# Causal attention: the next unit's transposes go ahead of the output projection on TensorE

## The chip, the cores and the metric

One NeuronCore of a Trainium2 chip runs the whole program. TensorE (PE) multiplies and transposes into PSUM, VectorE (DVE), ScalarE (ACT) and GpSimd (POOL) do the element-wise work, SyncE (SP) issues most DMAs. The engines run their own instruction streams in order and meet at semaphores. The metric is the device time in microseconds of one execution, the median of the runs.

## The reference, cut to what matters

A decoder of two layers with layer norms behind each sublayer, on x of 32 sequences x 128 rows x 256 features. Only the causal attention of the second layer is touched:

```
q = einsum('btm,mhd->bhtd', x, wq); k = ... wk; v = ... wv      # 2 heads of 128
q = frac_rope(q) * 128 ** -0.5;  k = frac_rope(k) * 128 ** -0.5
s = einsum('bhid,bhjd->bhij', q, k), masked above the diagonal
o = einsum('bhij,bhjd->bhid', softmax(s), v)
x = layernorm(x + einsum('bhid,hdm->bim', o, wo))
```

Before it stands x = layernorm(x + experts(x)): two gathered expert rows for each row, weighted and added, then the norm. This is done in the same stage.

## The kernel before

The program is a sequence of stages; each engine has one function per stage. The stage in question has `c_sync`, `c_gpsimd`, `c_tensor`, `c_scalar` and `c_vector`. The work is cut into 16 units (UNITS) of two sequences, 256 rows each. `pipelined` calls `step(t)` for t = 0 to 20 on every engine (lag 5; the steps 8 to 15 are two rounds of a loop with four steps in its body, the others are written out). In a step an engine works on several units at once: `t.at(k, UNITS)` is unit t - k, or nothing where there is none. The order of an engine's work is the order of the `if` blocks in its `step`, written out by hand; there is no planner.

Unit n goes through the stage like this. Step n: x2 is loaded (L1368) and POOL issues four gathers of expert rows (L1414). Step n+1: VectorE mixes them (L1599) into C["r"] and takes the moments; POOL takes the root (L1394, L1396); ScalarE writes the normalised rows C["x3"] (L1403, called in the u0 block; the u4 block uses the same line for the stage's result x4). Step n+2: TensorE turns x3 into bank 0 (`to_feature`, four transposes, L490), ScalarE copies them to C["x3F"] (L1532), TensorE projects queries (bank 1), keys (bank 2, both L1454) and values (bank 3, L1509); VectorE and POOL do the rope (L1592 to L1594, L1410), ScalarE copies the values (L1577). Step n+3: mask and scores (L1480, L1486), maximum (L1632), exponential (L1557), reciprocal of the sum (L1644), weights normalised (L1571). Step n+4: TensorE turns the weights (L1468), ScalarE copies them (L1536), weights times values (L1501, bank 6), ScalarE's copy C["oF"] (L1551), output projection (L1517, bank 7). Step n+5: VectorE adds the residual (L1609) and takes the moments, then root and ScalarE's normalised result, which SP stores.

So TensorE's order in a step is: turn of x3, turn of weights, queries, scores, keys, weights times values, values, output projection. ScalarE's is: copy of turned x3, copy of turned weights, x4, upper half of the queries (L1543), x3, oF, exponential, upper half of the keys (L1566), normalised weights, values. VectorE's is: residual and moments of the unit five back, mix and moments of the newest, rope of the queries, maximum, rope of the keys, reciprocal.

`done(eng, sem, u)` waits until unit u has passed the semaphore; the turn of x3 waits for `c_x3` (the rows) and for `c_x3F` of the unit before (bank 0 emptied), the copy L1532 for `c_x3T` (the turn) and for `c_v` of the unit before (x3F read).

Of the kernel before, what the change touches and what calls it, by code (L numbers as in the profile page):

```python
# [23 lines left out]
ACT = mybir.ActivationFunctionType  # L24
# [7 lines left out]
UNITS = B // UB  # L32
# [134 lines left out]
def pipelined(eng, count, lag, step, unroll=2, peel=0, first=0, tail=None):  # L167


    head = lag + 2  # L170
    head += (count - head) % unroll
    for t in range(first, head):
        step(Unit(0, t, unroll))
    with eng.Fori(0, (count - head - peel) // unroll) as i:
        for j in range(unroll):
            step(Unit(i, head + j, unroll))
    for t in range(count - peel, count + (lag if tail is None else tail)):
        step(Unit(0, t, unroll))


def done(eng, sem, u, per=1):

    if u.fixed and u.n < 0:
        return
    eng.wait_ge(sem, (u.n + 1) * per)
# [16 lines left out]
def decoder(nc, a, where, out):  # L202
    ctx = ExitStack()
    with ctx:
# [5 lines left out]
        def sem(name):  # L210
            in_use.append(nc.alloc_semaphore(name))
            return in_use[-1]
# [6 lines left out]
        def bank(k):  # L219
            return psum[:, k, :]  # L220
# [265 lines left out]
        def to_feature(dst, src):  # L486

            for c in range(NC_):
                for b in range(UB):
                    ins = nc.tensor.transpose(dst[:, c * T + b * S:c * T + (b + 1) * S],  # L490
                                              src[:, b, c * P:(c + 1) * P], ident)
            return ins
# [17 lines left out]
        def chunks(ap):  # L510
            return ap.rearrange("p (c t) -> p c t", c=NC_)
# [7 lines left out]
        def seqs(ap):  # L519
            return ap.rearrange("p (b d) -> p b d", b=UB)  # L520
# [775 lines left out]
        C = {}  # L1296
        for n in ("x2", "v", "x4"):
# [20 lines left out]
        c_idx, c_mix, c_x3T, c_q, c_k, c_v, c_S, c_pT, c_o, c_wo = (  # L1318
            sem("c_" + n) for n in ("idx", "mix", "x3T", "q", "k", "v", "S", "pT", "o", "wo"))
        c_x3F, c_q2, c_k2, c_vs, c_ex, c_pTs, c_os = (  # L1320
            sem("c_" + n) for n in ("x3F", "q2", "k2", "vs", "ex", "pTs", "os"))
# [4 lines left out]
        c_x3, c_x4 = ln3[3], ln4[3]  # L1326
# [15 lines left out]
        def kv_rest_tensor(pe):  # L1342
            for k in range(KV_REST):
                pe.wait_ge(kr_in[k], 16)
                done(pe, kr_s, Unit(0, k - 2), 2)
                project_features(bank(4 + 2 * (k % 2)), "L1_xattn_Wk", KV["cF_rest"][:, k])
                project_rows(bank(5 + 2 * (k % 2)), "L1_xattn_Wv", KV["cF_rest"][:, k]).then_inc(kr_p, 1)
            pe.wait_ge(kr_s, 2 * KV_REST)
# [97 lines left out]
        def c_tensor(pe):  # L1446
            kv_rest_tensor(pe)

            def project(u, k, name, s_out, read):
                for r in read:  # L1450
                    done(pe, r, u.back(1))
                for h in range(H1):
                    for c in range(NC_):
                        ins = nc.tensor.matmul(bank(k)[:, h * T:(h + 1) * T], w[name][:, c, h * P:(h + 1) * P],  # L1454
                                               C["x3F"][:, c, :], start=(c == 0), stop=(c == NC_ - 1))
                ins.then_inc(s_out, 1)

            def step(t):
                u1, u2, u3 = (t.at(k, UNITS) for k in (2, 3, 4))
                if u1:  # L1460
                    done(pe, c_x3, u1)
                    done(pe, c_x3F, u1.back(1))
                    to_feature(bank(0), C["x3"][:, u1.c % 4]).then_inc(c_x3T, 1)
                if u3:
                    done(pe, c_p, u3)
                    done(pe, c_pTs, u3.back(1))
                    for n in range(UB * H1):
                        ins = nc.tensor.transpose(bank(5)[:, n * S:(n + 1) * S], C["e"][:, u3.p, n, :], ident)  # L1468
                    ins.then_inc(c_pT, 1)
                if u1:  # L1470
                    done(pe, c_x3F, u1)
                    project(u1, 1, "L1_attn_wq", c_q, (c_qt, c_q2))
                if u2:
                    done(pe, c_qr, u2)
                    done(pe, c_kr, u2)
                    done(pe, c_q2, u2)
                    done(pe, c_k2, u2)
                    done(pe, c_ex, u2.back(1))

                    nc.tensor.matmul(bank(4), ident_bf[:, :],  # L1480
                                     causal_bf[:, None, :].broadcast_to([P, UB * H1, S]), start=True, stop=False,
                                     skip_group_check=True)
                    for b in range(UB):
                        for h in range(H1):
                            n = b * H1 + h
                            ins = nc.tensor.matmul(bank(4)[:, n * S:(n + 1) * S],  # L1486
                                                   C["q"][:, u2.p, h, b * S:(b + 1) * S],
                                                   C["k"][:, h, b * S:(b + 1) * S], start=False,
                                                   stop=(n == UB * H1 - 1), skip_group_check=True)
                    ins.then_inc(c_S, 1)  # L1490
                if t.fixed and t.n == UNITS + 2:
                    e_turn(pe, Unit(0, 0, 4), 0)
                if u1:
                    project(u1, 2, "L1_attn_wk", c_k, (c_kt, c_k2))
                if u3:
                    done(pe, c_pTs, u3)
                    done(pe, c_vs, u3)
                    done(pe, c_os, u3.back(1))
                    for b in range(UB):
                        for h in range(H1):  # L1500
                            ins = nc.tensor.matmul(bank(6)[:, h * T + b * S:h * T + (b + 1) * S],  # L1501
                                                   C["v"][:, u3.p, b, h * P:(h + 1) * P],
                                                   C["pT"][:, b * H1 + h, :], start=True, stop=True)
                    ins.then_inc(c_o, 1)
                if u1:
                    done(pe, c_vs, u1.back(1))
                    for b in range(UB):
                        for c in range(NC_):
                            ins = nc.tensor.matmul(bank(3)[:, b * D:(b + 1) * D], C["x3F"][:, c, b * S:(b + 1) * S],  # L1509
                                                   w["L1_attn_wv"][:, c, :], start=(c == 0), stop=(c == NC_ - 1))  # L1510
                    ins.then_inc(c_v, 1)
                if u3:
                    done(pe, c_r4, u3.back(1))
                    done(pe, c_os, u3)
                    for b in range(UB):
                        for h in range(H1):
                            ins = nc.tensor.matmul(bank(7)[:, b * D:(b + 1) * D], C["oF"][:, h, b * S:(b + 1) * S],  # L1517
                                                   w["L1_attn_wo"][:, h, :], start=(h == 0), stop=(h == H1 - 1))
                    ins.then_inc(c_wo, 1)
                if t.fixed and t.n == UNITS + 2:  # L1520
                    e_query(pe, Unit(0, 0, 4), 1)
            pipelined(pe, UNITS, C_LAG, step, unroll=4)

        def c_scalar(act):
            kv_rest_scalar(act)

            def step(t):
                u0, u1, u2, u3, u4 = (t.at(k, UNITS) for k in (1, 2, 3, 4, 5))
                if u1:
                    done(act, c_x3T, u1)  # L1530
                    done(act, c_v, u1.back(1))
                    nc.scalar.activation(C["x3F"], chunks(bank(0)), ACT.Copy).then_inc(c_x3F, 1)  # L1532
                if u3:
                    done(act, c_pT, u3)
                    done(act, c_o, u3.back(1))
# [38 lines left out]
                if u1:  # L1574
                    done(act, c_v, u1)
                    done(act, c_o, u1.back(2))
                    nc.scalar.activation(C["v"][:, u1.p], seqs(bank(3)), ACT.Copy).then_inc(c_vs, 1)  # L1577
                if t.fixed and t.n == UNITS + 2:
                    e_take_query(act, Unit(0, 0, 4), 1)
                if t.fixed and t.n == UNITS + 3:  # L1580
# [199 lines left out]
        def e_turn(pe, u, k):  # L1780
            landed(pe, x_in, u, 2)
            to_feature(bank(k), X["x4"][:, u.p]).then_inc(x_xT, 1)

        def e_query(pe, u, k):
            done(pe, x_xF, u)
            project_features(bank(k), "L1_xattn_Wq", X["x4F"]).then_inc(x_q, 1)
# [737 lines left out]
```

## Time and profile before

| | us |
|---|---|
| median of 3 runs (lowest to highest) | 1630.32 (1626.74 to 1630.99) |
| the profiled execution: time | 1628.0 |
| the profiled execution: span, first to last instruction | 1626.0 |

| engine | busy us in the span | share |
|---|---|---|
| PE (matmuls) | 1494.3 | 92% |
| DVE | 1123.7 | 69% |
| ACT | 823.3 | 51% |
| POOL | 603.2 | 37% |

The busy times cover six stages with different limits. The stage of the change fills roughly the stretch from 728 us (first turn of x3) to 924 us (last residual add), about an eighth of the span. Within it the idle time just before an instruction and what ended it (the groups, the timeline) say who waits for whom, and the chain of waits, followed back from the last instruction, says which of these waits are passed on to the end.

### The profile page before, as it was taken

Reading aid. Unit: us, or ns where it says so; the run is one execution under the profiler, and the core shown is the slowest. Engines: PE = TensorE matmul, PEld = TensorE weight load, DVE = VectorE, ACT = ScalarE, POOL = GpSimd, SP = SyncE. Lnnn points to the kernel's source line nnn. Section 1 sums busy time; section 2 is a strip of 40 time slices with the busy share of each in tenths; the row PEclk is TensorE's granted clock in tenths of the full one; section 3 lists DMA queues with packets and bytes.
Section 4 is the critical chain, followed back from the end, with each engine's and each line's share of the span. In section 5 each row is a group of like instructions: output and inputs, shape, how many; then the busy total and the mean of one; then the engine's idle time right before and its main releaser. Section 6 shows DMA issues by size and latency. Waiting matters only on the chain.

```text
span 1626.0 us, 34497 instructions
## 1 busy us (share of the span) xinstructions
PE 1494.3 (92%) x12742; PEld 1341.2 (82%) x12742; DVE 1123.7 (69%) x2334; ACT 823.3 (51%) x1559; POOL 603.2 (37%) x700
## 2 busy tenths in 40 slices
PE   4888889899999999978999789999979999989997
PEld 2777777799999999957778568888869999979997
DVE  3899987756555556317889448888766676757684
ACT  5777742245444544425777546656524444434442
POOL 3666651222012111027887213313114444434443
PEclk9999999899999999988999879999989999989999
DMA  6222253203233331062333132222136445363533
GB/s 192 66 79 77 71 189 109 97 27 101 95 104 103 97 97 40 14 210 79 94 91 115 58 133 80 70 68 77 35 75 126 99 102 125 84 126 68 118 76 73
DMA packets 118159, 152.11 MB, mean 94 GB/s; under 512 B 10090, under 2 KB 102852, under 8 KB 117508
## 3 DMA queue, kind: packets, MB, share of 16 engines
q1 hardware_dynamic: 110068, 127.48, 28.5%
q0 software_dynamic: 6560, 19.02, 4.1%
q10 hardware_dynamic: 1392, 3.70, 0.6%
q8 instruction: 94, 1.54, 0.4%
q14 instruction: 45, 0.37, 0.1%
HBM read 111.37 MB, written 38.80 MB: 92 GB/s over the span
## 4 chain that ended last, share of the span: by engine, by line
PE 36%; issue 7%; DVE 6%; DMA 3%; ACT 2%; POOL 2%; SPq 1%; DVEq 0%; POOLq 0%; ACTq 0%
PE psum L531 14%; PE psum L1880 4%; PE psum L506 3%; PE psum L498 3%; PE psum L1857 2%; PE psum L1454 2%; PE psum L1848 2%; DMA arena_x<-wT_d 1%; POOL d_g_parts L2236 1%; PE psum L1517 1%; PE psum L1835 1%; PE psum L1842 1%; PE psum L490 1%; PE psum L1509 1%; DVE psum L2465 1%
## 5 line engine op out<-in xcount | busy, mean ns | idle before, releaser
L2236 POOL TENSOR_TENSOR d_g_parts<-arena_w,d_g_parts 128x512 fp32r<-128x512 f32 x128 | 166.2, 1299 | 247.0 <-ACT d_g_parts L2368 246.8
L531 PE MATMUL psum<-d_v_high,d_g_parts 128*128 128x256 f32 x1024 | 205.5, 284 | 4.7 <-DVE arena_x L2006 3.2
L531 PE MATMUL psum<-d_x_parts,d_v_high 128*128 128x256 f32 x1024 | 194.4, 287 | 8.5 <-issue 7.1
L531 PE MATMUL psum<-m_w_high,m_h_parts 128*128 128x256 f32 x1024 | 188.0, 284 | 0.0
L1213 ACT ACTIVATE arena_x<-psum,b_e 128x512 f32<-128x512 f32 x128 | 88.3, 690 | 189.3 <-PE psum L531 88.8
L1141 POOL DMA_INDIRECT arena_x<-x_d,slot_row x64 | 67.1, 1049 | 293.0 <-PE psum L1187 228.5
L531 PEld LDWEIGHTS psum<-d_v_high,d_g_parts 128*128 128x128 f32 x1024 | 168.7, 192 | 5.5 <-issue 4.7
L531 PEld LDWEIGHTS psum<-d_x_parts,d_v_high 128*128 128x128 f32 x1024 | 160.0, 192 | 15.5 <-issue 9.7
L531 PE MATMUL psum<-m_xF_parts,m_w_high 128*128 128x512 f32 x512 | 159.5, 393 | 2.1 <-DVE m_xF_parts L526 2.1
L531 PEld LDWEIGHTS psum<-m_w_high,m_h_parts 128*128 128x128 f32 x1024 | 160.7, 192 | 0.0
L2376 ACT ACTIVATE arena_y<-psum 128x512 f32<-128x512 f32 x128 | 76.2, 596 | 152.7 <-PE psum L531 152.4
L2465 DVE SCALAR_TENSOR_TENSOR psum<-arena_y,psum 128x512 f32<-128x512 f32 x128 | 88.4, 691 | 87.3 <-ACT arena_y L2376 87.0
L531 PE MATMUL psum<-d_x_parts,d_vd_low 128*128 128x256 f32 x512 | 145.3, 284 | 0.0
L531 PE MATMUL psum<-d_vu_low,d_g_parts 128*128 128x256 f32 x512 | 145.3, 284 | 0.0
L531 PE MATMUL psum<-m_w_low,m_h_parts 128*128 128x256 f32 x512 | 144.8, 283 | 0.0
L2368 ACT ACTIVATE d_g_parts<-arena_w 128x512 fp32r<-128x512 f32 x128 | 80.4, 628 | 71.0 <-DVE arena_w L2471 71.0
L526 DVE TENSOR_TENSOR m_h_parts<-arena_x,m_h_parts 128x512 fp32r<-128x512 f32 x128 | 84.6, 686 | 43.8 <-ACT m_h_parts L1217 43.8
L531 PEld LDWEIGHTS psum<-m_xF_parts,m_w_high 128*128 128x128 f32 x512 | 96.0, 190 | 21.8 <-issue 2.5
L2471 DVE TENSOR_TENSOR arena_w<-psum,arena_x 128x512 f32<-128x512 f32 x128 | 88.4, 691 | 27.5 <-DMA arena_x<-wT_d 22.8
L1948 ACT ACTIVATE arena_x<-psum,arena_x 128x1024 f32<-128x1024 f32 x64 | 71.2, 1113 | 57.8 <-PE psum L1857 55.6
L531 PE MATMUL psum<-m_xF_parts,m_w_low 128*128 128x512 f32 x256 | 100.4, 392 | 0.0
L2031 DVE TENSOR_REDUCE arena_x<-psum 128x8 f32<-128x1024 f32 x64 | 78.0, 1220 | 29.9 <-PE psum L1848 29.8
(281 smaller groups left out, 3768.4 us busy)
## 6 DMA issues: line engine op xcount, KB each, us to landing
arena_x<-wT_d SPq DMA_DIRECT2D x128, 256.0 KB, 5.7
arena_y<-in_L_ffn_w SPq DMA_DIRECT2D x16, 1024.0 KB, 7.9
x_d<-arena_x SPq DMA_DIRECT2D x32, 256.0 KB, 2.2
y_d<-arena_x SPq DMA_DIRECT2D x16, 512.0 KB, 9.1
arena_x<-kv_d SPq DMA_DIRECT2D x16, 512.0 KB, 3.6
kv_d<-arena_x SPq DMA_DIRECT2D x9, 512.0 KB, 3.0
arena_x<-in_x SPq DMA_DIRECT2D x16, 256.0 KB, 2.9
arena_x<-in_ctx SPq DMA_DIRECT2D x16, 256.0 KB, 3.0
```

Of the source, the lines that this page charges most:

```text
L526: return nc.vector.tensor_tensor(dst, src, high.bitcast(F32), ALU.subtract)
L531: ins = nc.tensor.matmul(dst, left[a_], right[b_], start=start and k == 0, stop=stop and k == 2, skip_group_check=True)
L1141: nc.gpsimd.indirect_dma_start(out=M["x"][:, u.p, q, :], out_offset=None, in_=x2_d.rearrange("b s d -> (b s) d"), in_offset=bass.IndirectO ...
L1213: nc.scalar.activation(M["hr"][:, m % 4, :], bank(2 + m % 4), ACT.Relu, bias=b1_e[:, (u.c // 2) % 2, m:m + 1]).then_inc(m_hs, 1)
L1880: ins = nc.tensor.matmul(bank(7)[32 * quad:32 * quad + 32, (kind * NC_ + c) * S:(kind * NC_ + c + 1) * S], left, X["eT"][:, b, at:at + S], ...
L1948: nc.scalar.activation(X["eT"][:, b, half * 1024:(half + 1) * 1024].rearrange("p (q n) -> p q n", q=2), psum[:, 4:6, :], ACT.Exp, scale=HD ...
L2031: nc.vector.tensor_reduce(X["mx"][:, b, :].rearrange("p (q j) -> p q j", q=4)[:, quads_, 0:4], psum[:, quads_, :].rearrange("p q (k s) -> ...
L2236: nc.gpsimd.tensor_tensor(K["gP"][:, s % 4, 1], K["g"][:, s % 2], K["gP"][:, s % 4, 0].bitcast(F32), ALU.subtract).then_inc(d_gl, 1)
L2368: nc.scalar.activation(K["gP"][:, s % 4, 0], K["g"][:, s % 2], ACT.Copy).then_inc(d_gh, 1)
L2376: nc.scalar.activation(K["th"][:, s % 2], bank(2 + s % 4).rearrange("p (k t) -> p k t", k=2), ACT.Tanh, scale=0.5).then_inc(d_th, 1)
L2465: nc.vector.scalar_tensor_tensor(z, K["th"][:, s % 2].rearrange("p k t -> p (k t)"), 1.0, z, ALU.add, ALU.mult).then_inc(d_t, 1)
L2471: nc.vector.tensor_tensor(K["g"][:, s % 2], z, K["w"][:, s // 4, 2 * (s % 4):2 * (s % 4) + 2, :] .rearrange("p k t -> p (k t)"), ALU.mult) ...
```

## The change

On TensorE the block that turns x3 leaves the head of the step, where it served unit t - 2, and stands now behind the value projection and ahead of the output projection, where it serves unit t - 1. On ScalarE the block that copies the turned rows leaves the head of the step and stands behind the value copy, for unit t - 1. Each unit is thus turned and copied in step n+1 and not in step n+2. The waits are the same, of the same units. Buffers, banks, the other engines and all DMAs are as before.

```
@@ c_tensor, step(t)
-                u1, u2, u3 = (t.at(k, UNITS) for k in (2, 3, 4))
-                if u1:
-                    done(pe, c_x3, u1)
-                    done(pe, c_x3F, u1.back(1))
-                    to_feature(bank(0), C["x3"][:, u1.c % 4]).then_inc(c_x3T, 1)
+                u0, u1, u2, u3 = (t.at(k, UNITS) for k in (1, 2, 3, 4))
                 if u3:
                     done(pe, c_p, u3)
@@ behind the value projection
                     ins.then_inc(c_v, 1)
+                if u0:
+                    done(pe, c_x3, u0)
+                    done(pe, c_x3F, u0.back(1))
+                    to_feature(bank(0), C["x3"][:, u0.c % 4]).then_inc(c_x3T, 1)
                 if u3:
                     done(pe, c_r4, u3.back(1))
                     done(pe, c_os, u3)
@@ c_scalar, step(t)
-                if u1:
-                    done(act, c_x3T, u1)
-                    done(act, c_v, u1.back(1))
-                    nc.scalar.activation(C["x3F"], chunks(bank(0)), ACT.Copy).then_inc(c_x3F, 1)
@@ behind the value copy
                     nc.scalar.activation(C["v"][:, u1.p], seqs(bank(3)), ACT.Copy).then_inc(c_vs, 1)
+                if u0:
+                    done(act, c_x3T, u0)
+                    done(act, c_v, u0.back(1))
+                    nc.scalar.activation(C["x3F"], chunks(bank(0)), ACT.Copy).then_inc(c_x3F, 1)
```

## Rows read from the trace of the kernel before

**Rows 1.** Busy time of each engine, 740 to 895 us, TensorE's granted clock, DMA share, GB/s.

```profile
740.00:895.00 155.00, 141.69 (x772) 120.97 (x770) 134.81 (x375) 111.44 (x300) 122.52 (x169) 0.98 0.33 96
```

**Rows 2.** Groups, 740 to 895 us: busy us, mean ns | idle before us <-releasers.

```profile
L1454 PE MATMUL psum<-arena_y,arena_w 128*128 128x256 f32 x218 | 54.8, 395 | 5.3 <-ACT arena_y L1532 5.3
...
L1609 DVE TENSOR_TENSOR arena_y<-psum,arena_y 128x512 f32<-128x512 f32 x13 | 9.0, 691 | 8.4 <-PE psum L1517 8.4
L1468 PE MATMUL psum<-arena_w,arena_y 128*128 128x128 f32 x52 | 9.0, 298 | 8.0 <-ACT arena_y L1571 7.9
...
L1532 ACT ACTIVATE arena_y<-psum 128x512 f32<-128x512 f32 x13 | 7.7, 591 | 0.0
```

**Rows 3.** Chain of waits, 800 to 850 us: start us, us, what.

```profile
807.52 1.99 PE psum L1454 x8
...
809.73 0.89 PE psum L1486 x8
810.62 1.73 PE psum L1454 x8
812.35 0.89 PE psum L1501 x8
813.24 1.73 PE psum L1509 x8
814.97 1.74 PE psum L1517 x8
...
816.74 0.70 DVE arena_y L1609
...
826.95 0.19 DVE arena_y L1644
...
829.06 0.50 ACT arena_y L1532
...
829.60 1.99 PE psum L1454 x8
```

**Rows 4.** Chain of waits: three more starts of the query projection.

```profile
762.97 1.99 PE psum L1454 x8
...
852.02 1.99 PE psum L1454 x8
...
896.40 1.99 PE psum L1454 x8
```

**Rows 5.** Timeline, 811 to 820 us: start us, us, engine line [idle before <-releaser].

```profile
812.12 1.09 ACT L1403 ACTIVATE arena_y<-arena_y,C_st 128x256 f32<-128x256 f32 x2 [1.98 <-POOL C_st L1396]
...
813.28 0.60 ACT L1551 ACTIVATE arena_y<-psum 128x512 f32<-128x512 f32 x1
...
814.81 1.89 PE L1517 MATMUL psum<-arena_w,arena_y 128*128 128x256 f32 x8
...
816.54 0.60 PE L490 MATMUL psum<-arena_w,arena_y 128*128 128x128 f32 x4
...
817.49 0.66 PE L1468 MATMUL psum<-arena_w,arena_y 128*128 128x128 f32 x4 [0.35 <-ACT arena_y L1571]
817.96 0.59 ACT L1532 ACTIVATE arena_y<-psum 128x512 f32<-128x512 f32 x1
```

**Rows 6.** Timeline, 904 to 910 us: the four transposes between other matmuls.

```profile
907.72 0.60 PE L490 MATMUL psum<-arena_w,arena_x 128*128 128x128 f32 x4
...
908.16 1.06 PE L1501 MATMUL psum<-arena_y 128*128 128x128 f32 x8
```

**Rows 7.** Chain of waits, 878 to 965 us: the stage's end and the next stage's start.

```profile
903.85 1.74 PE psum L1517 x8
...
937.95 7.86 DMA arena_x<-kv_d
```

**Rows 8.** VectorE's mix L1599, 750 to 890 us: its idle time before, us, times, until.

```profile
L1599 DVE SCALAR_TENSOR_TENSOR arena_y<-arena_y,gates x51: 471/479/493, 749.6 to 886.6; 128x256 f32<-128x256 f32 x51
...
  issue: 1.1, 4
```

## Prediction

> **What bounds the kernel now.** The change touches one stage of six, the causal attention of the second layer, so I read that stage and not the shares of the whole span. Between 740 and 895 us TensorE is busy for 141.69 of 155 us at a mean granted clock of 0.98, VectorE for 134.81, POOL for 122.52, ScalarE for 111.44 [rows 1]. No engine is full, so the order decides, and the next view is the list of idle times. There the reader is to see four entries. VectorE waits 13 times, 8.4 us in all, for the last output projection matmul (L1517) before it can add the residual (L1609). TensorE waits 5.3 us for ScalarE's copy of the turned rows (L1532) before it projects the queries (L1454), and 7.9 us for the weights' normalisation (L1571) before it turns the weights (L1468). The copy L1532 itself waits for nothing: 0.0 us in 13 instances [rows 2]. So the thing that this change brings forward, the turn that feeds L1532, is not late in any of these steps.
>
> The chain of waits says how the waits join. It runs: query projection at 807.52, then scores, keys, P times V, values and output projection, each starting where the one before it ends, to 816.71 (814.97 + 1.74), VectorE's residual add at 816.74, then VectorE's queue in order (moments, mix of the gathered rows, rope products) to the reciprocal at 826.95, ScalarE's normalisation and value copy, its copy of the turned rows at 829.06, and query projection again at 829.60 [rows 3]. That is one round, 22.08 us, and it spans two steps: the projection of step t releases the queries of step t+2. Two such rounds are interleaved, one for even and one for odd steps. Other starts of the same line give the mean: from 762.97 to 896.40 there are 12 steps, 11.12 us each, so 22.24 us a round; 852.02 less 829.60 is 22.42 [rows 3, 4].
>
> **The change, part by part.** *TensorE.* The four transposes of a unit (L490) now stand behind the step's output projection; they go ahead of it. They were the first thing of step t+1 and become the last but one of step t, so on TensorE they move past exactly one thing, the eight matmuls L1517. Nothing is added or taken away, and no DMA or queue of SP or POOL is moved.
>
> What the turn costs where it stands: nothing. In the timeline the projection's eight matmuls begin at 814.81, the turn at 816.54, and after it TensorE idles 0.35 us until ScalarE's normalisation ends and L1468 can start at 817.49 [rows 5]. Taking the turn away from there gives nothing, since this wait is ended by ScalarE, not by TensorE's queue. The query projection behind it does not come sooner either: its copy L1532 starts at 817.96, right behind the value copy, whatever TensorE did [rows 5].
>
> What it costs in its new place: TensorE is gapless from the query projection to the end of the output projection [rows 3], so the projection ends later by the turn's length. Price of a turn between other matmuls: another turn of the same form, which stands between the scores and the value product, starts at 907.72 and the next matmul at 908.16, so 0.44 us for four [rows 6]. Bounds: four times 0.11 as just read, which I take, and 0.60, the turn's own busy time with its pipeline's end in it [rows 5]. The Trainium skill, "TensorE: Matmul & The Clock Gate", Part 4, puts a PE-mode transpose at about 275 ns in a kernel's context; that would be an estimated 1.1 us for a turn and 6.6 us in the sum below, and 1636.9 us in place of my time. This trace has a mean of about 0.27 us for the duration of one, but the next instruction starts 0.11 us later, and the sum goes by starts.
>
> *The turn's waits.* It waits for the next unit's normalised rows (L1403). In the step of rows 5 these two instructions start at 812.12 and take 1.09 us, so they end at 813.21, while the value projection hands over to the output projection at 814.97 [rows 3, 5]: 1.7 us of slack. Queued behind this wait is now the output projection, but that needs ScalarE's copy L1551 (813.28, 0.60 us), which stands behind L1403 in ScalarE's own order [rows 5]. So whatever holds the turn would hold the projection anyway; the wait adds nothing. The turn's other wait, that bank 0 has been emptied, is for a copy at the start of the same step.
>
> *ScalarE.* The copy goes from the head of step t+1 to the tail of step t. Between the value copy and the next copy (L1536) nothing else stands, so the order of its instructions over the stage is unaltered: value copy, turned rows, turned weights. It already starts without waiting [rows 2]. Gain and loss: 0. Only the place of the loop's back edge changes, between two instructions that follow each other without a gap.
>
> *The sum.* Steps with both a turn and a projection: the first output projection is in the fifth step (t = 4), the last turn in step t = 16, so 13 of the 16 turns are moved ahead of a projection. But a delay enters a round only once in two steps. The odd round passes the projections of t = 5, 7, 9, 11, 13, 15 and arrives at the last query projection (896.40) [rows 4]: 6 x 0.44 = 2.6 us. The even round passes seven, 3.1 us, and ends in a step where VectorE idles for the projection of the odd one. From there on no turn stands ahead of a projection and the 2.6 us are carried: projection at 903.85, then after the stage's last results the next stage's key and value loads at 937.95 [rows 7], both on the chain. Later stages are the same code.
>
> What can take a part of it off: VectorE's mix of the gathered rows starts late by 1.1 us in four instances between 750 and 890, by waits that the profile puts down to issue [rows 8]; where that is a gather still in flight, a round stretched elsewhere hides it. Shared by two rounds this is 0.5 to 1.1 us at most. I leave it out of the sum and keep it for the lower bound, 1.5 us.
>
> Profiled execution: span 1626.0 us, time 1628.0; with the change 1628.6 and 1630.6. The median of the three runs is 2.3 us above that profiled time, so the forecast is 1630.3 + 2.6 = 1632.9 us, 0.16% slower, which a measurement of this kernel cannot tell from no change (it tells about 0.3%, 4.9 us).
>
> **Rivals.**
> (a) *One-step round.* If VectorE's own sequence, or the turn of the weights, hands the delay on in each step and not in each second one, all 13 turns count: 13 x 0.44 = 5.7 us, 1636.0 us, slower. It decides from 0.38 us a step on (4.9 / 13). For it: VectorE is busy 134.81 of 155 us [rows 1], so few pauses are left in which its queue could catch up. Against it: it does pause, 8.4 / 13 = 0.65 us in every step right before the residual add [rows 2], and TensorE pauses before L1468 and L1454.
> (b) *Nothing moves.* The gathers, not the projection, set the pace: each gather waits for POOL, the mix waits for the gather, POOL waits for the mix, and this loop goes round in one step. If this loop sets the 11.12 us a step now and the two-step round has 0.22 us a step to spare, the delay vanishes in it: 1630.3 us. For it: the 1.1 us [rows 8]. Against: only four pauses in more than twelve steps, and the chain goes past them.
> (c) *The queries come sooner.* If the copy were released earlier by the turn, TensorE's 5.3 us before L1454 [rows 2] would go, all of it more than paying for the turn: 1630.3 - 5.3 = 1625.0 us, if the delay does not count as well. Against: L1532 has no idle time before it.
> (d) The turn costs more than 0.44 us between two long runs of 256-column matmuls: at 0.60 the sum is 3.6 us, 1633.9, at 1.1 us (four durations of a transpose) 6.6 us, 1636.9.
>
> **How the numbers follow.** Forecast, with (d) up to 0.6 us a turn: 0.60. (b): 0.14. (a), with the dearer (d) and a granted clock that falls in some other place: 0.19. (c): 0.07. Within 0.3% lie the forecast, (b) and the near ends of the others: 0.72. Slower by more: 0.20. Faster by more: 0.08. The range: below, (b) and the scatter of the three runs, which reach 3.6 us below their median, 1627.5; above, (a) and (d), 1637.0. What is left out are (c) and the tails.
>
> **What the profile will show.** If the steps are right: L490's four stand between L1509 and L1517; VectorE's idle time before L1609 grows; TensorE's before L1468 grows by less than 0.44 us a step; L1532 still idles 0.0; L1454's starts are about 11.34 us apart instead of 11.12; the stage's last query projection is 2.6 us later. The prediction is wrong if L1454's starts stay at 11.1 (b), go to 11.5 and more (a), or if L1454 no longer waits for L1532 (c).

## The result, and the profile after

The change makes the kernel a little slower: 1631.86 us (median of 20 runs, 1628.42 to 1643.15) against 1628.71 us (20 runs, 1623.52 to 1634.23); ratio 1.0028, 95% interval 1.0014 to 1.0041. The difference of the medians is 3.2 us, the ratio says 4.6 us; both are slower, and small. The forecast was 2.6 us slower (1632.9 us). The profiled execution has a span of 1630.9 us, 4.9 us above that of before.

In the tables of the changed kernel the value projection is L1505, the turn of the weights L1464, ScalarE's copy of the turned rows L1577, its value copy L1573, its normalisation L1567, its exponential L1553; the turn of the rows (L490) and the output projection (L1517) kept their numbers. First the chain of waits between 815 and 835 us, which answers to [rows 3] (start us, us, what):

```profile
817.44 0.97 ACT arena_y L1567 x3
...
818.43 0.60 ACT arena_y L1573
819.03 0.50 ACT arena_y L1577
...
819.57 1.99 PE psum L1454 x8
...
825.29 1.73 PE psum L1505 x8
827.02 0.44 PE psum L490 x4
827.46 1.74 PE psum L1517 x8
829.20 0.02 issue
829.23 0.70 DVE arena_y L1609
```

The reader is to see one new line, L490 x4 with 0.44 us, between the value projection and the output projection, on the chain. From the query projection's start to the projection's end it is 9.63 us (827.46 + 1.74 - 819.57) where it was 9.19 [rows 3]. What ScalarE does ahead of the query projection (normalisation, value copy, copy of the turned rows) is the same, in the same order. The groups between 740 and 900 us (busy, mean ns | idle before <-releaser) answer to [rows 2]:

```profile
L1454 PE MATMUL psum<-arena_y,arena_w 128*128 128x256 f32 x216 | 55.5, 402 | 5.6 <-ACT arena_y L1577 5.6
...
L1464 PE MATMUL psum<-arena_w,arena_y 128*128 128x128 f32 x56 | 9.6, 297 | 10.8 <-ACT arena_y L1567 10.4
L1609 DVE TENSOR_TENSOR arena_y<-psum,arena_y 128x512 f32<-128x512 f32 x13 | 9.0, 691 | 12.2 <-PE psum L1517 12.2
...
L1577 ACT ACTIVATE arena_y<-psum 128x512 f32<-128x512 f32 x14 | 8.3, 592 | 0.0
```

VectorE's wait for the output projection rose from 8.4 to 12.2 us (13 adds in both: 0.65 to 0.94 us each). TensorE's for the normalised weights rose from 7.9 us in 13 steps to 10.4 us in 14, 0.61 to 0.74 us each. The query projection still waits for the copy (5.6 us), and the copy, whose turn now comes early, still waits 0.0 us: it had nothing to gain.

One thing was not forecast. TensorE's part of the timeline between 838 and 848 us:

```profile
838.17 1.89 PE L1517 MATMUL psum<-arena_w,arena_y 128*128 128x256 f32 x8
841.22 0.65 PE L1464 MATMUL psum<-arena_w,arena_y 128*128 128x128 f32 x4 [1.16 <-ACT arena_y L1567]
842.43 3.31 PE L1454 MATMUL psum<-arena_y,arena_w 128*128 128x256 f32 x8 [0.56 <-ACT arena_y L1577]
845.54 0.63 PE L1476 MATMUL psum<-causal_bf,ident_bf 128*128 128x512 bf16 x1
```

The query projection of step 12 (unit 10) takes 3.31 us instead of 1.99. In the windows (stretch, its length, busy us of PE, PEld, DVE, ACT, POOL, granted clock, DMA share, GB/s) the clock of that stretch is 0.92:

```profile
740.00:762.00 22.00, 18.65 (x90) 15.35 (x89) 15.84 (x39) 12.90 (x38) 15.43 (x19) 0.84 0.25 73
828.00:850.00 22.00, 19.68 (x102) 16.25 (x101) 18.76 (x54) 14.11 (x35) 17.85 (x26) 0.92 0.32 91
```

In the kernel before the same stretch is granted 1.00:

```profile
828.00:850.00 22.00, 20.30 (x114) 17.39 (x113) 19.64 (x56) 16.23 (x44) 18.30 (x27) 1.00 0.34 96
```

I split each profiled execution at instructions whose first and last start a line's own view gives. "Steps 5 to 17" is the time from ScalarE's copy of the turned rows that the query projection of step 5 needs to the copy that step 17's needs, twelve periods; "stage" is from its first such copy to VectorE's last residual add (L1609); "next" from there to the first L2465 of the last stage; "last" from the first to the last L2465. All in us:

| kernel | steps 5 to 17 | one step | stage | next | last | span |
|---|---|---|---|---|---|---|
| before | 133.42 | 11.12 | 194.2 | 275.3 | 412.4 | 1626.0 |
| the change | 137.92 | 11.49 | 197.6 | 275.3 | 414.2 | 1630.9 |

Of the 4.9 us the stage has 3.4: 4.5 in the twelve steps, and 1.0 back behind the last of them, from 27.8 to 26.8 us. That 1.0 us is one instruction group, the stage's last output projection, which runs at half clock for its whole length before (granted clock 0.50 between 919.77 and 923.50 us) and for a part of it after the change (0.68 between 923.81 and 926.60 us; first line before, second line the change):

```profile
919.77 3.75 PE L1517 MATMUL psum<-arena_w,arena_y 128*128 128x256 f32 x8 [2.91 <-ACT arena_y L1551]
923.81 2.79 PE L1517 MATMUL psum<-arena_w,arena_y 128*128 128x256 f32 x8 [2.91 <-ACT arena_y L1547]
```

The stage of the change also begins 0.4 us sooner in its profiled execution. Another 1.8 us are in the last stage, which the change does not touch and which differs from one profiled kernel to the next (below).

### The profile page after: what moved, and what is told of

It is laid out like the page before. It is cut to its first block, busy times and chain, and to the rows that moved or that the text cites. A ratio compares the mean times of both kernels' runs of the same rounds, so it can differ in the third digit from the quotient of the medians.

```text
span 1630.9 us, 34503 instructions
## 1 busy us (share of the span) xinstructions
PE 1494.4 (92%) x12742; PEld 1339.6 (82%) x12742; DVE 1125.1 (69%) x2334; ACT 822.1 (50%) x1559; POOL 602.4 (37%) x700
## 4 chain that ended last, share of the span: by engine, by line
PE 36%; DVE 7%; issue 5%; DMA 4%; ACT 2%; POOL 2%; SPq 1%; DVEq 0%; ACTq 0%; POOLq 0%
PE psum L531 14%; PE psum L1880 4%; PE psum L506 3%; PE psum L498 3%; DMA arena_x<-wT_d 2%; PE psum L1857 2%; PE psum L1454 2%; PE psum L1848 2%; DVE psum L2465 1%; PE psum L490 1%; PE psum L1835 1%; PE psum L1842 1%; PE psum L1517 1%; DMA wT_d<-arena_w 1%; PE psum L1505 1%
## 5 line engine op out<-in xcount | busy, mean ns | idle before, releaser
L531 PEld LDWEIGHTS psum<-d_x_parts,d_v_high 128*128 128x128 f32 x1024 | 160.2, 193 | 16.2 <-issue 10.4
L2465 DVE SCALAR_TENSOR_TENSOR psum<-arena_y,psum 128x512 f32<-128x512 f32 x128 | 88.4, 690 | 87.2 <-ACT arena_y L2376 87.0
```

What stands on the lines that cost most here:

```text
L531: ins = nc.tensor.matmul(dst, left[a_], right[b_], start=start and k == 0, stop=stop and k == 2, skip_group_check=True)
L2465: nc.vector.scalar_tensor_tensor(z, K["th"][:, s % 2].rearrange("p k t -> p (k t)"), 1.0, z, ALU.add, ALU.mult).then_inc(d_t, 1)
```

## The experiments

All ratios are against runs of the kernel before on the same chip, with their 95% intervals. In the kernels called filled, TensorE does transposes that nobody uses, in every step or (early) in the first steps alone; they are explained below, under the granted clock.

| kernel | time, ratio (interval) | steps 5 to 17 | one step | stage | next | last |
|---|---|---|---|---|---|---|
| TensorE's part alone | 1.0022 (1.0004 to 1.0040) | 137.96 | 11.50 | 197.7 | 275.3 | 413.4 |
| ScalarE's part alone | 1.0001 (0.9985 to 1.0016) | 133.44 | 11.12 | 194.1 | 275.4 | 417.6 |
| the turn three times | 1.0023 (1.0005 to 1.0042) | 141.69 | 11.81 | 198.9 | 276.7 | 407.8 |
| projection ahead of values | 1.0010 (0.9993 to 1.0028) | 136.45 | 11.37 | 197.3 | 275.4 | 410.7 |
| copy ahead of values | 0.9980 (0.9966 to 0.9994) | 133.77 | 11.15 | 191.4 | 272.6 | 413.2 |
| queries first | 0.9946 (0.9932 to 0.9959) | 130.94 | 10.91 | 188.1 | 272.3 | 411.7 |
| change, filled | 1.0040 (1.0025 to 1.0054) | 136.27 | 11.36 | 194.6 | 276.9 | 414.7 |
| before, filled | 0.9944 (0.9927 to 0.9961) | 133.43 | 11.12 | 191.7 | 272.3 | 407.7 |
| before, filled early | 0.9912 (0.9890 to 0.9933) | 133.45 | 11.12 | 191.8 | 272.2 | 408.0 |
| change, filled early | 0.9972 (0.9956 to 0.9988) | 136.27 | 11.36 | 194.6 | 272.6 | 408.6 |
| queries first, filled early | 0.9910 (0.9893 to 0.9928) | 130.17 | 10.85 | 186.0 | 278.1 | 406.2 |

### The two halves of the change

TensorE's block moved, ScalarE's left, and the other way round.

> Only TensorE's part of the change: the turn for unit t-1 ahead of the output projection, ScalarE's copy at the head of its step as before. Theory (the turn lengthens a round that spans two steps): same as the whole change, 2.6 to 3.1 us above before, query projections 11.36 us apart where the granted clock stays full, first query projection with an output projection in the step before it to the last one 3.0 us longer than before's 133.4 us. Rival (ScalarE's copy at its new place costs something): 0 to 1 us above before.

> Only ScalarE's part: the copy of the turned rows stands behind the value copy of the step before, TensorE as before. Theory: ScalarE's instructions follow each other in the same order, so 0 us, within 0.5 us of before, query projections 11.12 us apart. Rival (the place of the copy counts): it carries a good part of the 3 us.

The first gives 137.96 us for the twelve steps, the change 137.92; the second 133.44, before 133.42. The cost is TensorE's alone and ScalarE's move is worth nothing. The first shows the slow step 12 as well, with the granted clock at 0.92 between 828 and 850 us, so this is no accident of one execution. The times agree with it: ratio 1.0022 for TensorE's half, 1.0001 for ScalarE's.

### A larger dose: the turn three times

```
                 if u0:
                     done(pe, c_x3F, u0.back(1))
+                    to_feature(bank(0), C["x3"][:, u0.c % 4])
+                    to_feature(bank(0), C["x3"][:, u0.c % 4])
                     to_feature(bank(0), C["x3"][:, u0.c % 4]).then_inc(c_x3T, 1)
```

> The whole change, with the four transposes done three times over in the same place (eight transposes more in each step, the result is the same). Each step's output projection ends another 0.88 us later. Theory (two-step round): 6 x 0.88 = 5.3 us above the change, 8 to 9 us above before, query projections 11.36 + 0.44 = 11.8 us apart. Rival (a), every step passes the delay on: 13 x 0.88 = 11.4 us above the change, 12.2 us apart. Rival (b), the gathers set the pace: under 2 us above the change. If TensorE's own work becomes the limit (about 9.6 + 0.9 us and its two waits) the time lies between theory and rival (a).

TensorE's timeline (here L1519 is the output projection), one step, and the window around the first steps:

```profile
815.14 1.89 PE L1505 MATMUL psum<-arena_w,arena_y 128*128 128x256 f32 x8
816.87 1.47 PE L490 MATMUL psum<-arena_w,arena_y 128*128 128x128 f32 x12
818.18 1.89 PE L1519 MATMUL psum<-arena_w,arena_y 128*128 128x256 f32 x8
```

```profile
740.00:762.00 22.00, 19.08 (x113) 16.77 (x114) 16.79 (x41) 13.08 (x39) 17.27 (x23) 1.00 0.25 73
```

Twelve transposes take 1.31 us between starts, 0.11 each. A step takes 11.81 us, what the two-step round says (11.80), and not 12.2: rival (a) falls, and so does (b), since the gathers do not hide the growth. (11.80 is 11.36, a step of the change at full clock, and half of 0.88.) Yet the whole is hardly slower than the change, where 5.3 us more were expected. With the added transposes the granted clock is also higher in the first steps, 1.00 instead of 0.84, so the period of step 4 to 5 is 10.84 us and not 13.18, that of step 2 to 3 is 7.44 and not 8.31, and step 12 is not slow. The dose's cost, 5.4 us, stands in the steps, and a gain of another kind, 2.3 + 0.9 + 1.65 us, stands against it; with 0.8 us more behind the last step, the stage is 1.3 us longer than the change's. The last stage of this execution is 6.4 us shorter than the change's, in code that is the same. Judged by the time alone this run would have spoken for rival (b).

### The output projection ahead of the values

Kernel before, the two blocks exchanged on TensorE.

> The kernel before, with the output projection ahead of the value projection: the 1.73 us of the value projection leave the round, but the projection then waits for ScalarE's copy, which ends 0.6 us behind the product that it copies. Theory: the projection ends about 1.0 us sooner, 6 rounds, 5 to 6 us faster than before, unless the value projection, now last, holds ScalarE's value copy up (its slack is about 0, so 3 to 4 us are the lower estimate). Rival (a): 13 x 1.0 = 13 us faster at most. Rival (b): no change.

```profile
826.54 0.60 ACT L1551 ACTIVATE arena_y<-psum 128x512 f32<-128x512 f32 x1 [0.88 <-PE psum L1501]
827.28 1.97 PE L1510 MATMUL psum<-arena_w,arena_y 128*128 128x256 f32 x8 [0.78 <-ACT arena_y L1551]
829.08 1.89 PE L1517 MATMUL psum<-arena_w,arena_y 128*128 128x256 f32 x8
831.01 0.60 ACT L1577 ACTIVATE arena_y<-psum 128x512 f32<-128x512 f32 x1 [0.55 <-PE psum L1517]
```

Here L1510 is the output projection and L1517 the value projection. My lower estimate, 3 to 4 us gained, was wrong: steps take 11.37 us, regular, and the time is the same within its interval. The projection now waits 0.78 us for ScalarE's copy, and ScalarE's value copy 0.55 us for TensorE, which it never did before. That closes a round of one step: value projection, value copy, copy of the turned rows, query projection, and TensorE's queue through ScalarE's copy L1551 and the output projection back to the value projection. It takes 11.37 us, longer than half of the old two-step round (11.12). The slack that I had called about 0 was what decided.

### What the earlier turn makes possible

ScalarE copies the turned rows ahead of the values (first kernel), and ahead of the normalised weights, with TensorE's query projection ahead of its turn of the weights (second kernel):

```
 c_scalar, first kernel               c_scalar, second kernel
   normalised weights (u2)            + copy of turned rows (u0)
 + copy of turned rows (u0)             normalised weights (u2)
   value copy (u1)                      value copy (u1)
 - copy of turned rows (u0)           - copy of turned rows (u0)
 c_tensor, second kernel
 + queries (u1)
   turn of weights (u3)
 - queries (u1)
```

> The whole change, and ScalarE copies the turned rows ahead of the values (the turn is now ready by then). Theory (two-step round, ScalarE's value copy lies in it): 0.5 us less for a round, so the query projections are 11.36 - 0.25 = 11.1 us apart where the clock is full, 3.0 us less than the change, about the time of before, 0 to 1.5 us above it. Rival (the query projection is held by something else, the turn of the weights on TensorE): as the change.

> The whole change, and ScalarE copies the turned rows ahead of the normalised weights, and TensorE projects the queries ahead of the turn of the weights, so that the query projection hangs on the turn of the rows and no longer on the softmax. Theory: the query projection leaves the round (about 2 us less of 22.7), until another bound shows: VectorE's own step of 10.5 us or TensorE's own 10.1 us. Query projections 10.6 to 10.8 us apart, the stage 5 to 8 us shorter than before, 1622 to 1625 us. Rival (a one-step round through ScalarE shows up, as in the kernel with the output projection ahead of the values): 11.1 to 11.4 us apart, no gain.

The first: 11.15 us a step, 0.21 less than the change at full clock (11.36), 0.25 expected. The time was expected 0 to 1.5 us above the kernel before and came out 3.2 us below it, ratio 0.9980. The steps 5 to 17 do not give that (133.77 us against 133.42). In the profiled execution 2.3 us come in the steps before them, 0.9 us behind them and 2.7 us in the unchanged next stage. The period of step 4 to 5 is 11.46 us where the change has 13.18, and the query projection of step 4 takes 2.82 us where it takes 3.78 in the kernel before and in the change, with the granted clock at 0.92 and not 0.84 between 740 and 762 us, though nothing was filled in:

```profile
751.42 2.82 PE L1454 MATMUL psum<-arena_y,arena_w 128*128 128x256 f32 x8
```

The second, between 762 and 890 us and in its timeline (L1567 is the copy of the turned rows, L1467 the turn of the weights, L1571 the normalisation):

```profile
L1454 PE MATMUL psum<-arena_y,arena_w 128*128 128x256 f32 x188 | 45.7, 386 | 7.9 <-ACT arena_y L1567 7.9
...
L1532 ACT ACTIVATE arena_y<-psum 128x512 f32<-128x512 f32 x11 | 6.6, 597 | 10.1 <-PE psum L1467 10.1
```

```profile
823.20 0.60 ACT L1567 ACTIVATE arena_y<-psum 128x512 f32<-128x512 f32 x1
...
823.69 1.27 ACT L1571 ACTIVATE arena_y<-arena_y 128x128 f32<-128x128 f32 x4
823.85 1.99 PE L1454 MATMUL psum<-arena_y,arena_w 128*128 128x256 f32 x8 [0.54 <-ACT arena_y L1567]
...
825.68 0.60 PE L1467 MATMUL psum<-arena_w,arena_y 128*128 128x128 f32 x4
```

The query projection starts beside the normalisation, not behind it, and the turn of the weights finds them ready. 10.91 us a step (10.6 to 10.8 expected) and 1618.9 us (1622 to 1625 expected), ratio 0.9946: faster than both kernels. The stage is 6.1 us shorter than before's; 2.5 of that are in the twelve steps, the rest in the first steps, where the clock is better too (0.92), and 3.0 us more are in the unchanged next stage. The move that cost 2.8 us by itself stands here in a kernel whose steps are shorter than before's, once what stands behind the turn is moved up with it. Whether that gain needs the turn's new place was not tested: no run moves the copy and the query projection and leaves the turn where it was. What now remains is again a wait for the copy, 7.9 us over the window, and ScalarE's pause of 10.1 us for the turned weights.

### The granted clock

Unused turns into bank 5 behind the place of the output projection. Filled: one in each step that has a turn and three in the steps below 4; filled early: three in the steps below 4 alone. In the kernel before the condition is u1, so its first filled step is step 2, in the change (u0) it is step 1; the doses of the first steps differ by that.

```
                     ins.then_inc(c_wo, 1)
+                if u0:                       # filled early: and t.fixed and t.n < 4
+                    for _ in range(3 if t.fixed and t.n < 4 else 1):
+                        to_feature(bank(5), C["x3"][:, u0.c % 4])
```

> The whole change, with one more turn (four transposes, not used) behind the output projection in each step, three in the first steps, where TensorE waits anyway. Theory (of the change's 4.4 us in the stage 3.0 are the turn ahead of the projection and 1.4 a stretch at half the granted clock in step 12): the clock is 1.00 from 762 us on, the stretch goes, the query projections stay 11.36 us apart, and the half clock near 750 us goes too, as in the kernel with three turns: stage 3 to 5 us shorter than the change's, time near or below before's. Rival (the clock has nothing to do with it): no gain against the change, or a loss of up to 0.4 us a step.

> The kernel before with the same filling behind its output projection, for the turn alone at equal clock. Theory: 11.12 us apart as before, half clock near 750 us gone, stage 2 to 3 us shorter than before's, and shorter than the filled change by the turn's 2.6 to 3.0 us. Rival: filling costs TensorE 0.44 us a step and the pauses don't cover it, 0 to 3 us slower than before.

> The kernel before with three unused turns behind the place of the output projection in the first steps (t < 4) alone, where TensorE stands and the granted clock falls. Theory: step 4's queries at full clock, query projections then 11.12 us apart; attention stage 191.7 us against 194.2. If the whole time falls by far more than these 2.5 us, as it did with filling in every step (9.9 us), the rest lies in the stages behind, and the trace says in which; rival: the rest was the filling of the later steps, and this kernel gains 2.5 us only.

> The whole change with the same filling in the first steps alone. Theory (the stretch at half clock in step 12 belongs to the change's longer pauses in the later steps): it stays, query projections 11.49 us apart on average, stage 195.5 to 196.5 us, 4 to 4.5 us longer than with the filled kernel before. Rival (that stretch depends on what happened near 750 us): it goes or moves, 11.36 us apart, stage 194.6 us.

> The kernel with the queries ahead of the turn of the weights, and the filling in the first steps. Theory: its steps are 10.85 us apart at full clock already, so only the first steps gain: 0.5 to 2 us in the stage, 186 to 187.5 us; whole time 1617 to 1619 us, the fastest. Rival (the filling delays the first copies): as without it.

The two windows of the change, filled early:

```profile
740.00:762.00 22.00, 18.91 (x115) 16.31 (x114) 17.13 (x41) 11.78 (x35) 17.87 (x24) 1.00 0.26 82
828.00:850.00 22.00, 19.68 (x111) 16.64 (x111) 19.01 (x55) 15.71 (x44) 17.86 (x26) 1.00 0.32 92
```

With filling 137.92 becomes 136.27 us for the change, and before stays at 133.43 to 133.45. So at a full clock (1.00 in every window of 22 or 23 us from 740 to 895 us, in all four filled kernels) the turn's place costs 2.8 us, and the slow step 12 another 1.65 us. That step does not belong to the change's longer pauses in the later steps, as I had expected of the early filling: filling the first steps alone removes it. So it depends on what came before it. The filling also shifts the later steps in time, and no run separates the two; which part decides is not settled.

The filling of the first steps of the kernel with the queries first gives a stage of 186.0 us (186 to 187.5 expected) and 1616.6 us (1617 to 1619). Its stage is 5.8 us shorter than that of the kernel before filled early, and yet the two have the same ratio, 0.9910 and 0.9912: the next stage is 5.9 us longer in its profiled execution. By the whole time, then, no reordering that I ran is clearly faster than the kernel before with a few unused transposes.

The whole times do not follow the stage. The stage of the filled kernel before is about 2.5 us shorter, its time 9.9 us (11.8 with early filling); the filled change's stage is 3.0 us shorter than the change's and its time is not (ratio 1.0040, where near or below the kernel before was expected). The table shows where: the next stage takes 272 to 278 us and the last 406 to 418, in code that is the same in all kernels. In the last stage the waits for the spread weights (who waited <- for whom: us, times, longest) differ; between 1200 and 1625 us the kernel before, the filled change, the filled kernel before and the kernel before filled early have

```profile
DVE arena_w L2471 <- DMA arena_x<-wT_d: 22.8, 11, 5.0
```

```profile
DVE arena_w L2474 <- DMA arena_x<-wT_d: 43.7, 14, 5.1
```

```profile
DVE arena_w L2474 <- DMA arena_x<-wT_d: 14.1, 10, 4.9
```

```profile
DVE arena_w L2474 <- DMA arena_x<-wT_d: 41.0, 15, 4.2
```

They do not explain the stage's length: with 14.1 us of them it is 407.7 us long, with 41.0 us 408.0.

One profiled execution each can't tell a kernel's own habit from the scatter of single runs. That the runs with filling of the kernel before lie together (1611 to 1623 us in two kernels, 12 runs) speaks for a habit; why the stages behind gain 7 to 9 us by it stays open.

## Why the prediction was right

*The bound.* Right: a round of two steps through the output projection, VectorE's queue and ScalarE. The dose shows it: 8 more transposes, 0.88 us, lengthen a step by 0.45 us (141.69 us less the 136.27 of the filled change, which has the full clock too, is 5.42 us in twelve steps; 6 x 0.88 = 5.3). Rivals (b) and (c) fall as well: the steps did lengthen, and the query projection still waits for the copy.

*Removing the turn from its old place gains nothing, ScalarE's move costs nothing.* Right: the second half alone gives 133.44 us against 133.42, and L1577 idles 0.0 us.

*The price of 0.44 us and six rounds.* Right: L490 has 0.44 us on the chain, and at a full clock the twelve steps take 2.8 us more where 2.6 was the sum; a step is 11.36 us where the forecast was 11.34. The duration of a transpose is not what an instruction costs in a row of them: one takes about 0.27 us, twelve took 1.31 us. The prediction's other estimate, 6.6 us, was worked out from the duration of about 275 ns that the Trainium skill gives ("TensorE: Matmul & The Clock Gate", Part 4); the trace agrees with the duration, and the sum by it did not come.

*The wait for the normalised rows.* Right: the turn starts at 827.02 where the value projection ends (825.29 + 1.73), without a pause.

*What the sum lacked.* The slow step 12, 1.65 us. It stood in the prediction only as "a granted clock that falls in some other place", a part of rival (a)'s chance. The seen 11.49 us a step is 11.36 and this one step. Another effect of the clock, 1.0 us at the stage's last output projection, went the other way. The stage's last query projection came 4.0 us later (900.44 against 896.40 us), where the prediction's sign said 2.6: 4.5 us of the steps, less the 0.4 us by which the stage began sooner. The absorption by gathers, 0.5 to 1.1 us kept for the lower bound, did not show.

*Sign and size.* Within 0.3% by the ratio, at its edge: 1.0028 is 4.6 us, the medians give 3.2, the stage of the profiled execution 3.4, and the mechanism 2.8. That the whole time lies so near the sum is in part luck: 1.65 us for step 12, 1.0 us back at the stage's end, and stages behind that differ between kernels by more than the forecast, were not in it. What bears the account are the twelve steps.

## What to carry to other kernels

Before moving an instruction ahead, ask whether its consumer ever waits for it, and what it is moved ahead of: here the copy behind the turn had no idle time, and the thing it overtook was on a round that sets the pace. Count how many steps a round spans, since a delay enters only once for each time round. And if a producer is moved up, try its consumer with it: the same move together with two others gave a kernel 0.5% faster than before, 6.1 of the 9.0 us in this stage. Judge an experiment by the steps it aims at as well as by the total, because the clock and later stages can hide an effect of its size.

## What the runs showed of the hardware that was not expected

With unused transposes in the steps where TensorE waits, the granted clock there was 1.00 and not 0.84 (740 to 762 us), one period was 2.3 to 2.4 us shorter, and a slow step 90 us later was gone. So a stretch whose pauses are filled with transposes of 128 x 128 held the full clock here. The Trainium skill ("TensorE: Matmul & The Clock Gate", Part 4) says that the full rate does not engage in transpose mode, since a transpose does not count as busy in the same way; these windows speak against it. They do not prove how a transpose counts, for the clock of these first steps moves by other changes too: with the copy ahead of the values, and no transpose more, it is 0.92. And stages with unchanged code differed by up to 6 us (272.2 to 278.1) and 11 us (406.2 to 417.6) between the kernels' profiled executions.
